# A window-attention and two-expert block on one core: 64x64 products, gates spread by DMA, GpSimd sharing the gate products, and a new order of every engine

## The chip, the cores and the metric

The kernel runs on one core of a Trainium2 chip. The time is the device time of one execution in microseconds (us); lower is better. TensorE (PE), VectorE (DVE), ScalarE (ACT), GpSimd (POOL) and SyncE (SP, which here issues every DMA) each take their own list of instructions in order, and wait for each other through semaphores.

## The reference

The input x is 4 images of 64 channels, 128 by 128, float32. Two layers follow each other, both with a residual.

```
x = x + conv(ln_c(x))            # attention in windows of 8x8 tokens, 4 heads of 16 channels
    qkv  = ln_c(x)^T @ w_qkv.T
    attn = softmax(q k^T / 4 + bias[head])        # 64x64 for each window and head
    out  = (attn v) @ w_proj.T + b_proj
t = t + ffn(ln_t(t))             # t: x by tokens
    p = softmax(ln_t(t) @ router_w + router_b); the two largest, scaled to sum to one
    out = sum over the two of p_k * (ln_t(t) @ expert_w[e_k] + expert_b[e_k])
```

There are 8 experts of 64 by 64. No token is gathered: all 8 experts are applied to every token, each with the token's gate (zero for six of them).

## The kernel before, in words

A strip is 8 rows of two images: 64 channels of image 0 on partitions 0 to 63, of image 1 on 64 to 127, and 1024 tokens, which are 16 windows of 64 tokens. There are 32 strips. Each has two halves (chunks) of 512 tokens. The kernel is a software pipeline written out by hand: one step works on four strips at once (`pre`, `att`, `old`, `moe` at lines 526, 1004 and their like: normalisation with queries and keys, attention, router, experts), every step has 16 slots, and each engine has its own table of what to do in which slot. `steps` (line 232) writes out the first 7 steps, runs a loop of 6 rounds with 4 steps each, and writes out the last ones.

What one strip takes on each engine:

- **Queries and keys.** `split_product` (462): for each of the two and each half, three products 128x128x512 in fp32r, high and low parts of the input against high and low parts of the weights. ACT makes the high part (633), POOL the low part (774).
- **Scores.** `scores` (374, 378), for each of 8 units of two windows: the bias as one fp32r product of 512 columns, and two fp32 products of 256 columns. The weights on 128 partitions hold queries of both images in a block form (`qbd`), the keys are spread over four masked copies (`kex`, made by DVE at 996). Each unit has a PSUM bank of its own, two in all (banks 0 and 1).
- **Softmax.** DVE takes the row maximum (879) and subtracts (882), 512 columns at a time, ACT takes the exponent (587), PE transposes (388), ACT copies back (595), PE multiplies with the values (404) and with ones (410), ACT turns the sums into inverses (602, 604), DVE normalises (889).
- **Projection** (417), residual on POOL (767), router (436, 439), transposes of the logits (446).
- **Top two.** DVE does both picks in a chain of small instructions (`pick`, 920 to 924, and around it), then POOL splits the gates into bf16 parts (791 to 811), PE transposes them (455), DVE copies them to `gT` (1045).
- **Experts.** For each of 16 items (2 halves, 4 expert pairs, 2 images) PE spreads two rows of gates over 128 partitions with a bf16 product of 512 columns (`gates_wide`, 502), DVE multiplies this PSUM bank with `xd` (899; `xd` is the strip with one image on both halves of the partitions, copied by four DMAs at 319), and PE multiplies with two experts at once (`experts`, 514: 128 rows, 64 columns of the array). The two images sit on the two column halves of the array. The expert bias is two bf16 products (511), `finish` (907) adds the residual, and one DMA stores the strip (325).

Every matrix product of an ordinary fp32 operand shows as two matmul records and two weight loads in the trace, one of fp32r or bf16 as one.

## Time and profile before

| | |
|---|---|
| median of 3 runs | 1445.26 us (1443.87 to 1445.51) |
| span of the profiled execution | 1442.2 us |
| busy: PE, PEld (weight loads) | 1343.6 us (93%), 749.6 us |
| busy: DVE | 1161.9 us (81%) |
| busy: ACT | 862.6 us (60%) |
| busy: POOL | 356.8 us (25%) |
| DMA | 72.89 MB, queue q1 17.6% of 16 engines |

The span is what the profiler saw of one execution, from the first instruction to the last; the run's time is some 3 us longer. Busy times overlap across engines. A group "x1024 | 284.7, 621" says that 1024 instructions kept the engine busy for 284.7 us together while one took 621 ns: matmuls are pipelined, and those on different columns of the array overlap. What a group costs on the path is therefore better read from the chain of waits, in which each piece is given from its start to the start of what came next.

### The profile page before, as it was taken

How to read it: one execution, taken by the hardware profiler on the slowest of the kernel's cores; microseconds unless marked ns; L12 is line 12 of the kernel's file. 1: busy time of each engine (PE TensorE's matmuls, PEld its weight loads, DVE VectorE, ACT ScalarE, POOL GpSimd, SP SyncE). 2: the span in 40 equal slices, each digit the busy share in tenths (PEclk: the TensorE clock that was granted, in tenths of full speed). 3: DMA queues.
4: the chain of work that ended last, by engine and by line, in shares of the span. 5: the costliest groups of instructions: out<-in, count | busy, mean ns of one | idle time of the engine just before them, and what ended most of it. 6: DMA issues, size and time to landing. Idle time of an engine off the chain costs nothing.

```text
span 1442.2 us, 32800 instructions
## 1 busy us (share of the span) xinstructions
PE 1343.6 (93%) x11179; PEld 749.6 (52%) x11332; DVE 1161.9 (81%) x2398; ACT 862.6 (60%) x1729; POOL 356.8 (25%) x488
## 2 busy tenths in 40 slices
PE   5779999999998999989999999989999899999987
PEld 3555555555554555555555555545555555555531
DVE  4468888888887888878888788878888788888774
ACT  2576666566665666656666566656666566666530
POOL 2013222331232232122233132222123223213221
PEclk6899999999999999999999999999999999999998
DMA  4011211212221211221121222121222121221110
GB/s 156 1 45 30 60 40 50 60 31 60 60 60 32 60 45 45 60 61 45 45 60 31 60 60 59 35 57 30 60 60 60 31 60 40 51 60 45 45 44 30
DMA packets 20931, 72.89 MB, mean 51 GB/s; under 512 B 3600, under 2 KB 3856, under 8 KB 20624
## 3 DMA queue, kind: packets, MB, share of 16 engines
q1 hardware_dynamic: 20752, 70.60, 17.6%
q8 instruction: 101, 1.65, 0.5%
q14 instruction: 78, 0.64, 0.1%
HBM read 20.25 MB, written 16.78 MB: 26 GB/s over the span
## 4 chain that ended last, share of the span: by engine, by line
PE 69%; ACT 10%; DVE 10%; issue 9%; POOL 1%; DMA 1%; DVEq 0%; ACTq 0%; SPq 0%; POOLq 0%
PE bank L378 14%; PE bank L514 12%; PE bank L388 7%; PE bank L462 6%; PE bank L502 5%; ACT vbd L680 5%; PE bank L417 4%; PE bank L374 4%; PE bank L404 4%; DVE z L899 3%; PE bank L410 2%; PE bank L491 2%; PE bank L484 2%; PE bank L436 2%; DVE mx L879 2%
## 5 line engine op out<-in xcount | busy, mean ns | idle before, releaser
L899 DVE TENSOR_TENSOR z<-bank,xd 128x512 f32<-128x512 f32 x512 | 329.2, 683 | 15.4 <-PE bank L502 9.3
L514 PE MATMUL bank<-z,wcen 128*64 128x512 f32 x1024 | 284.7, 621 | 4.6 <-issue 0.3
L587 ACT ACTIVATE probs<-shifted 128x512 f32<-128x512 f32 x256 | 161.5, 631 | 208.0 <-DVE shifted L882 205.7
L378 PE MATMUL bank<-kex,qbd 128*128 128x256 f32 x1024 | 269.2, 386 | 0.0
L879 DVE TENSOR_REDUCE mx<-bank 128x8 f32<-128x512 f32 x256 | 176.1, 688 | 108.9 <-PE bank L378 107.4
L378 PEld LDWEIGHTS bank<-kex,qbd 128*128 128x128 f32 x1024 | 198.8, 194 | 25.6
L767 POOL TENSOR_TENSOR tt<-prj,xs 128x512 f32<-128x512 f32 x64 | 81.2, 1268 | 457.6 <-DVE z L899 287.9
L882 DVE TENSOR_TENSOR shifted<-bank,mx 128x512 f32<-128x512 f32 x256 | 177.1, 692 | 9.8
L388 PE MATMUL bank<-cst,probs 128*128 128x128 f32 x1024 | 157.7, 277 | 24.9 <-issue 16.8
L595 ACT ACTIVATE pt<-bank 128x512 f32<-128x512 f32 x256 | 150.7, 589 | 46.0 <-PE bank L388 43.0
L388 PEld LDWEIGHTS bank<-cst,probs 128*128 128x128 f32 x1024 | 124.5, 142 | 77.2 <-issue 38.9
L404 PEld LDWEIGHTS bank<-pt,vbd 128*32 128x32 f32 x4096 | 72.4, 109 | 153.8 <-issue 143.5
L502 PE MATMUL bank<-gT,select 128*128 128x512 bf16 x359 | 139.9, 393 | 11.0 <-DVE z L899 6.0
L774 POOL TENSOR_TENSOR xr_low<-xr,xr_high 128x512 fp32r<-128x512 f32 x64 | 81.6, 1274 | 224.9 <-ACT xr_high L633 224.9
L996 DVE TENSOR_SCALAR kex<-kr,cst 128x512 f32<-128x512 f32 x256 | 123.8, 546 | 8.1 <-ACT kr L669 7.1
L502 PEld LDWEIGHTS bank<-gT,select 128*128 128x128 bf16 x512 | 49.4, 98 | 150.7 <-issue 102.9
L374 PE MATMUL bank<-bias_hl,tile_id 128*128 128x512 f32 x256 | 124.2, 485 | 0.7 <-DVE bias_hl L872 0.7
L680 ACT ACTIVATE vbd<-bank 64x256 f32<-64x256 f32 x256 | 96.7, 378 | 32.9 <-PE bank L491 27.3
L404 PE MATMUL bank<-pt,vbd 128*32 128x64 f32 x4096 | 109.6, 225 | 1.0 <-DVE onrm L889 0.8
L791 POOL TENSOR_TENSOR ga<-oh,g 128x128 f32<-128x128 f32 x32 | 13.0, 406 | 367.9 <-DVE g L964 367.9
L514 PEld LDWEIGHTS bank<-z,wcen 128*64 128x64 f32 x1024 | 53.2, 135 | 88.8 <-DVE z L899 43.4
L640 ACT ACTIVATE qbd<-bank 64x512 f32<-64x512 f32 x128 | 75.2, 587 | 16.0 <-PE bank L462 14.4
(116 smaller groups left out, 1998.2 us busy)
## 6 DMA issues: line engine op xcount, KB each, us to landing
xd<-tt SPq DMA_DIRECT2D x128, 256.0 KB, 4.0
xs<-in_x SPq DMA_DIRECT2D x32, 512.0 KB, 4.8
out<-ob SPq DMA_DIRECT2D x32, 512.0 KB, 3.1
kex<-in_rel SPq DMA_DIRECT2D x1, 2048.0 KB, 9.4
tt<-in_select SPq DMA_DIRECT2D x1, 512.0 KB, 8.9
cst<-in_consts SPq DMA_DIRECT2D x1, 359.0 KB, 2.8
tt<-in_weights SPq DMA_DIRECT2D x1, 336.0 KB, 3.1
wproj<-in_proj SPq DMA_DIRECT2D x1, 64.0 KB, 8.2
```

Of the source, the lines that this page charges most:

```text
L374: mm(b, tile_id[:, :], dup(bias_hl[:, :, :].rearrange("p h k -> p (h k)")), start=True, stop=False, skip_group_check=True)
L378: last = mm(b[:, 256 * j:256 * j + 256], qbd[s.buf(2)][:, w, :, :].rearrange("p a q -> p (a q)"), kex[s.buf(2)][:, w, :, :].rearrange("p h ...
L388: last = nc.tensor.transpose(bank[:, PT_BANK, 128 * j:128 * j + 128], probs[u % 2][:, j // 2, 128 * (j % 2):128 * (j % 2) + 128], cv("ident"))
L404: last = mm(bank[q:q + 32, OD_BANK, N * w4:N * w4 + N], vbd[s.buf(2)][:, 2 * u + wl, q:q + 32], pt[g % 2][:, w4, j, a, :], start=True, sto ...
L502: mm(bank[:, G_BANK[n % 2], :], select[:, 4 * a + j, :], gT[s.buf(2)][:, c * CH:(c + 1) * CH], start=True, stop=True).then_inc(g_full, 1)
L514: mm(bank[64 * a:64 * a + 64, Y_BANK, :], wcen[:, WE + C * j:WE + C * j + C], z[n % 4][:, :], start=False, stop=(j == 3), skip_group_check ...
L587: af(probs[u % 2][:, :, :].rearrange("p w k -> p (w k)"), shifted[u % 2][:, :, :].rearrange("p g k -> p (g k)"), ACT.Exp).then_inc(exp_don ...
L595: af(pt[g % 2][:, 2 * (u % 2):2 * (u % 2) + 2, :, :, :].rearrange("p w j a q -> p (w j a q)"), bank[:, PT_BANK, :], ACT.Copy).then_inc(pt_ ...
L680: af(dst[:, :, :, h, :], src[:, :, :, h, :], ACT.Copy).then_inc(v_ready, 1)
L879: red(mx[u % 2][:, :], b, axis=AX_X, op=ALU.max).then_inc(max_done, 1)
L882: tt_(shifted[u % 2][:, :, :], b, mx[u % 2][:, :].unsqueeze(2).broadcast_to([P, 8, N]), op=ALU.subtract).then_inc(shift_done, 1)
L899: tt_(z[n % 4][:, :], bank[:, G_BANK[n % 2], :], xd[s.buf(2)][:, a, c * CH:(c + 1) * CH], op=ALU.mult).then_inc(z_ready, 1)
```

## The change

Almost every instruction is rewritten. What it does:

- **64x64 products.** `wcen`, `wproj` and the new `wex` are used in 64x64 blocks. `swapped` (queries and keys), `project` and `experts` each issue four products of 64 rows, 64 columns and 512 columns of data, one for each quarter of the array, with the two row halves writing different banks. Queries and keys are plain fp32: the split into high and low parts is gone, and with it the instructions on ACT and POOL.
- **Scores.** `kex` and `qbd` go. The queries come out with the windows' halves on the partitions; products of 32 rows and 64 columns, 128 columns of data, go to two banks (the "two score banks" are now one pair, filled by a left half, `scores_left`, and after it a right half, `scores_right`, which uses the other row groups). ACT writes the keys in two masked copies (`move_k`) where DVE wrote four.
- **Softmax** works on four groups of 1024 columns in place of eight units of 512. It is done in place in `probs`.
- **Gates by DMA.** Three transposes of 128 columns replace eight. ACT copies them to `gsb`, a DMA writes them to a DRAM buffer `gates_dram`, and for each expert two DMAs read one row into 64 partitions of `gz`. `gates_wide` is gone. Six small DMAs bring rows for the expert bias (`grow`).
- **Gate products.** `gz` times the strip, 128x1024 with both inputs in SBUF, eight for each strip: experts 1, 4 and 7 on POOL, the other five on DVE. There is one `gz` buffer for each expert, so an expert's next gates are loaded when its product is done.
- **Order.** Eight pipeline stages in place of four, one written list for each engine and step (39 steps for 32 strips; 11 written out, a loop of 5 rounds with 4 steps, 8 written out).
- **Store.** `ob` now has image-independent halves, stored with four DMAs whose runs are 64 numbers (256 bytes) long; `xd` gives way to `tx`, half as large.

```diff
+            def write_gates(s):
+                sp.wait_ge(gsb_ready, s.count(1, 1))
+                sp.dma_start(gates_dram[s.buf(4)].rearrange("s r (x p) -> (r x) s p", p=P),
+                             gsb[:, :, :]).then_inc(gates_written, 16)
+            def load_gate_rows(s):
+                sp.wait_ge(gates_written, s.count(16, 16))
...
+            def spread_gates(s, e):
+                wait(sp, e_done, s.count(E, e + 1, lag=1))
+                for a in range(2):
+                    sp.dma_start(gz[64 * a:64 * a + 64, e, :],
+                                 gates_dram[s.buf(4), 0, E * a + e, :].partition_broadcast(64)
+                                 ).then_inc(gz_loaded[e], 16)
...
-                for w, v in ((0, 1), (1, 0), (0, 0)):
-                    last = mm(bank[:, PRE, :], wqk_hl[w][:, at:at + P], chunk(xr_hl[v], c), start=(w, v) == (0, 1),
-                              stop=(w, v) == (0, 0), skip_group_check=True)
+                for x in range(2):
+                    for a in range(2):
+                        last = mm(bank[64 * x:64 * x + 64, PRE + a, :], wcen[64 * a:64 * a + 64, at + 64 * a:at + 64 * a + 64],
+                                  xr[s.buf(2)][64 * a:64 * a + 64, x, :, :].rearrange("p w n -> p (w n)"),
+                                  start=True, stop=True)
...
+                        for hp in range(2):
+                            r = 2 * x + hp
+                            last = mm(bank[N * j:N * j + N, S_BANK + hp, 256 * x + 128 * ii:256 * x + 128 * ii + 128],
+                                      qs[32 * r:32 * r + 32, a, w, :],
+                                      km[32 * r:32 * r + 32, CW * a + w, :, :].rearrange("p m k -> p (m k)"),
+                                      start=False, stop=(ii == 1), skip_group_check=True)
...
-                mm(bank[:, G_BANK[n % 2], :], select[:, 4 * a + j, :], gT[s.buf(2)][:, c * CH:(c + 1) * CH],
-                   start=True, stop=True).then_inc(g_full, 1)
...
-                mm(bank[64 * a:64 * a + 64, Y_BANK, :], wcen[:, WE + C * j:WE + C * j + C], z[n % 4][:, :],
-                   start=False, stop=(j == 3), skip_group_check=True).then_inc(e_done, 1)
+                for x in range(2):
+                    for a in range(2):
+                        last = mm(bank[64 * x:64 * x + 64, Y_BANK + a, :], wex[64 * a:64 * a + 64, e, :],
+                                  gz[64 * a:64 * a + 64, e, x * CH:(x + 1) * CH],
+                                  start=False, stop=(e == E - 1), skip_group_check=True)
+                last.then_inc(e_done, 1)
...
+        POOL_Z = [1, 4, 7]
+        DVE_Z = [e for e in range(E) if e not in POOL_Z]
...
+            def gated(s, e):
+                dve.wait_ge(gz_loaded[e], s.count(32, 32))
+                tt_(gz[:, e, :], gz[:, e, :], tt[s.buf(4)][:, :, :].rearrange("p x t -> p (x t)"),
+                    op=ALU.mult).then_inc(z_dve, 1)
```

The order on TensorE, in the middle of a step of the kernel before. L388 are the transposes, L374 and L378 the scores of one unit, L502 a spread of gates, L514 a pair of expert products, L484 a spread of the inverse deviations, L404 and L410 values and denominators:

```order
L388 MATMUL bank<-cst,probs 128x128 x4
L374 MATMUL bank<-bias_hl,tile_id 128x512
L378 MATMUL bank<-kex,qbd 128x256 x2
L502 MATMUL bank<-gT,select 128x512
L514 MATMUL bank<-z,wcen 64x512 x2
L484 MATMUL bank<-var_hl,spread 128x512
L404 MATMUL bank<-pt,vbd 32x64 x8
L410 MATMUL bank<-pt,cst 32x256 x4
L502 MATMUL bank<-gT,select 128x512
```

And with the change, from the expert bias on (L581). L593 are the products of one expert (x4) or three (x12), L437 keys and then queries, L491 and L476 bias and one half of the scores of a group:

```order
L581 MATMUL bank<-grow,eb 128x512 x2
L428 MATMUL bank<-var_hl,spread 128x512 x2
L509 MATMUL bank<-cst,probs 128x128 x4
L476 MATMUL bank<-km,qs 64x128 x8
L593 MATMUL bank<-gz,wex 64x512 x4
L437 MATMUL bank<-xr,wcen 64x512 x4
L593 MATMUL bank<-gz,wex 64x512 x12
L437 MATMUL bank<-xr,wcen 64x512 x4
L526 MATMUL bank<-pt,vbd 32x64 x16
L509 MATMUL bank<-cst,probs 128x128 x4
L533 MATMUL bank<-pt,cst 32x256 x4
```

No spread of gates stands between the experts any more, and experts, keys and queries of the same shape now follow each other.

The end of a step on VectorE with the change. L1000 and L1007 are maximum and subtraction, L1021 a gate product (experts 0 and 2 at the end, of the strip whose gates were made in this step), L1015 the normalisation, and L975 and L980 (the variance) open the next step:

```order
L1021 TENSOR_TENSOR gz<-gz,tt 128x1024
L1015 TENSOR_TENSOR onrm<-bank,rden 128x256
L1021 TENSOR_TENSOR gz<-gz,tt 128x1024
L1000 TENSOR_REDUCE mx<-bank 128x16
L1007 TENSOR_TENSOR probs<-bank,mx 128x1024
L1021 TENSOR_TENSOR gz<-gz,tt 128x1024
L975 TENSOR_TENSOR var<-bank,msq 64x512
L980 TENSOR_SCALAR var<-var 64x512
```

Before, a gate product read a PSUM bank that PE filled; now it reads what a DMA has written, and the maximum of the third score group is queued behind one.

One step on SyncE with the change (before, it issued six DMAs: `xs`, four `xd`, `out`). The write at L304 waits for the gates of this step, the six rows at L312 for that write:

```order
L340 DMA out<-ob 64x8x64 x4
L329 DMA tx<-tt 64x512 x4
L304 DMA gates_dram<-gsb 128x3x128
L312 DMA grow<-gates_dram 8x2x512 x6
L320 DMA gz<-gates_dram 64x1024 x8
L299 DMA xs<-in_x 128x1024
L320 DMA gz<-gates_dram 64x1024 x8
```

The first eight `gz` are experts 0 to 3 of the strip just routed, the last eight (experts 4 to 7 of the same strip) belong to the next step.

## Rows read from the trace of the kernel before

**Rows 1.** The page: span, busy time, slices and TensorE's granted clock.

```profile
span 1442.2 us, 32800 instructions
PE 1343.6 (93%) x11179; PEld 749.6 (52%) x11332; DVE 1161.9 (81%) x2398; ACT 862.6 (60%) x1729; POOL 356.8 (25%) x488
PEclk6899999999999999999999999999999999999998
q1 hardware_dynamic: 20752, 70.60, 17.6%
```

**Rows 2.** Stretches of one step: busy us (instructions) of each engine, clock, DMA.

```profile
666.60:708.20 41.60, 40.54 (x344) 22.86 (x346) 35.79 (x74) 26.86 (x55) 11.24 (x16) 1.00 0.19 52
708.20:749.80 41.60, 40.73 (x345) 22.77 (x347) 35.79 (x74) 27.00 (x56) 11.06 (x16) 1.00 0.19 52
```

**Rows 3.** Chain in order of time: start us, us until the next, what.

```profile
722.22 0.21 PE bank L502
722.44 1.01 PE bank L514 x4
...
723.88 0.36 PE bank L404 x16
724.24 0.43 PE bank L410 x8
724.67 0.55 PE bank L484
725.22 0.44 PE bank L388 x4
725.66 0.23 PE bank L374
725.89 0.86 PE bank L378 x4
...
731.79 0.59 PE bank L511 x2
732.38 1.01 PE bank L514 x4
733.39 0.89 PE bank L462 x3
```

**Rows 4.** The same chain before and at a return of the loop.

```profile
445.68 0.90 PE bank L491 x8
...
448.87 3.48 issue
452.35 0.67 PE bank L388 x4
453.03 0.43 PE bank L374
453.45 1.71 PE bank L378 x4
```

**Rows 5.** Groups of instructions by line and shape: DVE and ACT, and POOL's.

```profile
L899 DVE TENSOR_TENSOR z<-bank,xd 128x512 f32<-128x512 f32 x512 | 329.2, 683 | 15.4 <-PE bank L502 9.3 <-remote 2.9 <-DVE oh L924 1.1
L889 DVE TENSOR_TENSOR onrm<-bank,rden 128x256 f32<-128x256 f32 x128 | 53.1, 414 | 5.4 <-ACT rden L604 5.3
L921 DVE TENSOR_TENSOR eq<-L,m 128x128 f32<-128x128 f32 x64 | 18.7, 292 | 3.0 <-DVE m L920 1.0
L604 ACT ACTIVATE rden<-rden 128x256 f32<-128x256 f32 x128 | 53.4, 417 | 4.1
L587 ACT ACTIVATE probs<-shifted 128x512 f32<-128x512 f32 x256 | 161.5, 631 | 208.0 <-DVE shifted L882 205.7
L767 POOL TENSOR_TENSOR tt<-prj,xs 128x512 f32<-128x512 f32 x64 | 81.2, 1268 | 457.6 <-DVE z L899 287.9 <-ACT prj L690 169.7
L791 POOL TENSOR_TENSOR ga<-oh,g 128x128 f32<-128x128 f32 x32 | 13.0, 406 | 367.9 <-DVE g L964 367.9
L795 POOL TENSOR_TENSOR gp<-ga,gb 128x128 bf16<-128x128 f32 x32 | 21.6, 674 | 0.0
```

**Rows 6.** Timeline of SP's own queue: start us, us for the issues.

```profile
0.75 0.40 SPq L286 DMA_DIRECT2D cst<-in_consts  x1
...
5.24 0.64 SPq L306 DMA_DIRECT2D tt<-in_select  x1
```

**Rows 7.** DMA groups: KB each, median us from issue to landing.

```profile
xd<-tt SPq DMA_DIRECT2D x128, 256.0 KB, 4.0
cst<-in_consts SPq DMA_DIRECT2D x1, 359.0 KB, 2.8
```

**Rows 8.** Timeline: start us, us, engine; DVE and POOL side by side.

```profile
702.11 2.23 DVE L996 TENSOR_SCALAR kex<-kr,cst 128x512 f32<-128x512 f32 x4
719.21 1.67 DVE L996 TENSOR_SCALAR kex<-kr,cst 128x512 f32<-128x512 f32 x4
...
702.20 0.71 POOL L795 TENSOR_TENSOR gp<-ga,gb 128x128 bf16<-128x128 f32 x1
1411.16 0.45 POOL L795 TENSOR_TENSOR gp<-ga,gb 128x128 bf16<-128x128 f32 x1
```

**Rows 9.** Timeline of the setup, DVE and PE: one-hot tables, bias products, bias.

```profile
12.52 4.62 DVE L844 TENSOR_SCALAR xd<-kex,cst 128x4096 bf16<-128x4096 int32 x2 [2.48 <-DMA kex<-in_rel]
17.19 1.03 PE L347 MATMUL bank<-tb,xd 128*64 128x12 bf16 x32 [7.25 <-DVE xd L844]
35.74 0.28 DVE L867 COPY probs<-bank 128x128 f32<-128x128 f32 x1
37.99 0.42 DVE L872 TENSOR_TENSOR bias_hl<-probs,bias_hl 64x256 fp32r<-64x256 f32 x1
```

More of the change, by code:

```diff
@@ L224, in __init__, with strips @@
                 self.c, self.n, self.inner = c, n, inner
-            def strip(self, off):
-                return Strip(self.c + off, self.n, self.inner)
+            def strips(self):
+                return [Strip(self.c - k, self.n, self.inner) for k in range(LAST_STAGE + 1)]
         class Strip:
@@ L255, in steps @@
         def steps(run):
-            first, last = -1, STRIPS + 1
-            lo = 6
-            n = (STRIPS - 1 - lo) // U
-            for i in range(first, lo):
+            last = STRIPS - 1 + LAST_STAGE
+            lo = LAST_STAGE + 4
+            n = (STRIPS - lo) // U
+            for i in range(lo):
                 run(Step(i, 0, False))
@@ L314, in _ @@
[L314 to L325 removed]
+                s = st.strips()
@@ new lines, in score_tiles @@
+            def score_tiles(s, g, x):
+                a = g // 2
+                for ii in range(2):
+                    for j in range(2):
+                        w = 4 * (g % 2) + 2 * ii + j
+                        for hp in range(2):
[4 more added lines that the diff above has]
+                                      start=False, stop=(ii == 1), skip_group_check=True)
+                return last
@@ new lines, in _ @@
+                s = st.strips()
+                if s[7].on:
+                    experts(s[7], 7)
+                if s[4].on:
+                    values(s[4], 1)
+                if s[5].on:
+                    router(st, s[5])
+                if s[4].on:
+                    denominators(s[4], 0)
+                    transposes(s[4], 2)
+                if s[5].on:
+                    transpose_logits(st, s[5])
+                if s[4].on:
+                    scores_left(s[4], 3)
+                if s[6].on:
+                    expert_bias_rows(s[6])
@@ new lines, in _ @@
+                if s[3].on:
+                    spread_std(st, s[3])
+                if s[4].on:
+                    transposes(s[4], 3)
+                    scores_right(s[4], 3)
+                if s[6].on:
+                    experts(s[6], 0)
+                if s[3].on:
+                    keys(st, s[3])
+                if s[6].on:
+                    experts(s[6], 1)
+                    experts(s[6], 2)
+                    experts(s[6], 3)
+                if s[3].on:
+                    queries(st, s[3])
@@ new lines, in _ @@
+                if s[6].on:
+                    experts(s[6], 4)
+                if s[4].on:
+                    project(st, s[4])
+                if s[3].on:
+                    scores_right(s[3], 2)
+                    transposes(s[3], 1)
+                    values(s[3], 0)
+                if s[2].on:
+                    channel_sums(st, s[2])
+                if s[6].on:
+                    experts(s[6], 5)
+                    experts(s[6], 6)
+                if st.c == 0:
+                    bias_rows()
```

1131 lines of the change are left out of this document (570 added, 561 removed).

## The prediction

> **What bounds the kernel now.** I read the page first: PE is busy 93% of the span, DVE 81%, and TensorE's granted clock is at 0.9 or more of its full 2.4 GHz in all but the first slices [rows 1]. Then the stretches of single steps: a step is 41.6 us, of which PE is busy 40.5 to 40.7, DVE 35.8, ACT 26.9, POOL 11.1 [rows 2]. Then the chain in order of time, in which piece follows piece on PE with no wait between [rows 3]. The kernel is bound by PE's own work. As a check, all the work of one strip, priced from the chain. Scores are 8 x (0.23 + 0.86) = 8.7, transposes 8 x 0.44 = 3.5, values and denominators 8 x 0.36 + 4 x 0.43 = 4.6, queries and keys 4 x 0.89 = 3.6, expert pairs 8 x 1.01 = 8.1, 16 spreads of gates at 0.21 (0.27 with changes of shape) = 4.3, two bias pairs 1.2; I add 7.7 for the rest (values' input 2 x 0.90 [rows 4] = 1.8, projection 2.0, deviations 1.0, router 1.0, sums 0.9, transposes of logits and gates 1.0). Together 41.7, against 41.6 measured. So the pieces of the chain are prices that add up to the step.
>
> At a return of the loop there are 3.48 us without an issue, and the scores behind it take 1.71 in place of 0.86, half the clock [rows 4]. Such a return costs some 4.9 us more than another step.
>
> **PE after the change.** I take the price of a piece of 512 fp32 columns from the pair L514, two products on different columns of the array: 1.01 us for both [rows 3]. L378, which has as many columns of data in a row (two products of 256), takes 0.86, so 0.15 of the 1.01 is the change of shape. The decisive unknown is what four products on the quarters cost. No product before uses fewer than 128 rows, so this trace does not show row halves side by side. Bounds: as the column halves do (0.86 for four), or one row half after the other (1.72 for four). I take the first, because the nearest row is a pair of column parts that run fully beside each other, and the two row halves here write different banks; the second is a rival below.
>
> - Eight experts, keys, queries and projection: 11 fours. In the new order experts 0 to 3 stand around keys and queries, 4 beside projection, 5 to 7 together, so three of them pay 1.01 and eight 0.86: 9.9 us.
> - Scores: four groups of two bias products (0.46) and two halves. A half is eight products of 128 columns on four parts of the array, two after each other, as many columns as L410 (0.43), plus 0.15 for the shape: 1.16. Together 6.5.
> - Unchanged: transposes 3.5, values and denominators 4.6, router 1.0, sums 0.9, logits' transposes 0.4, and 2.0 for the values' input (now 32 small products). 12.4.
> - Deviations 0.7, three gate transposes 0.35, expert bias as fp32r 0.6: 1.6. The spreads of gates are gone.
>
> The sum is 30.4 us for a strip.
>
> **DVE, ACT, POOL after the change.** From 256 to 512 columns a DVE instruction grows from 414 to 683 ns [rows 5], 1.05 ns a column, so 1024 columns are 1.22 us. DVE has 15 of these (5 gate products, 4 maxima, 4 subtractions, scaling, finish) = 18.3, four normalisations 1.7, variance 1.8, and the chain of some 22 small instructions at 0.17 to 0.29 with the waits between them, 6.5: 28.3 us. ACT grows by 0.84 ns a column (417 to 631), 1.06 for 1024: 12 of them 12.5, eight copies of 512 4.7, the rest 7.5: 24.7. POOL: (1268 - 406)/384 = 2.24 ns a column, so a gate product is 2.4 us; three, two residuals and seven-tenths of the old gate work (3.1) are 12.8. None of these sums exceeds PE's, but DVE is close behind.
>
> **DMA.** Before, 70.6 MB took 17.6% of 1442 us [rows 1], 3.6 us for a MB. Per strip there will be 16 x 0.262 (gates) + 3 x 0.52 (load, `tx`, store) + 0.3 = 6.1 MB: 22 us, no bound. The price lies in the latency. SP issues 32 DMAs in a step, and each keeps its queue for 0.40 to 0.64 [rows 6]; I take 0.45. The new stores have runs of 256 bytes, which no row shows; nothing waits for a store but `ob` two steps later, so they cost nothing on the path, and 2 us of DMA time even at half the rate.
>
> **The new path.** DVE's list is a ring: from the top of a step through the top-two picks and the gates, then out through POOL, PE, ACT and DMA, and back into DVE at the gate product of expert 0, behind which stands the third group's softmax and expert 2. Its length:
>
> 1. DVE from the variance to the gates, all that is queued there: 14.8 of work (five 1.22, variance 1.8, normalisation 0.4, the small chain 6.5) and 1.2 of waits for ACT and PE: 16.
> 2. POOL places the gates 3.1, three transposes with their latency 0.55, ACT's copy 0.55: 4.2.
> 3. The write to DRAM until it has landed, by the nearest small load [rows 7]: 2.8.
> 4. Six row loads and two spreads issued, 8 x 0.45 = 3.6, and landing. `xd`, of the same size, has 4.0 from issue; the bound below is 2.8 [rows 7]. I take 3.0 behind the last issue: 6.6.
> 5. Gate product, maximum, subtraction, gate product: 4.9.
>
> That is 34.5 us, longer than PE's 30.4. One more thing is added. DVE's new gate products have two inputs in SBUF, as has POOL's. In the trace DVE's four L996, SBUF to SBUF, took 2.23 us while POOL worked and 1.67 when it did not, and POOL's L795 0.71 against 0.45 [rows 8]: the two hold each other up. POOL will be busy 12.8 of some 35 us. Bounds: nothing, or that each DVE instruction of this kind waits for half of a 2.4 us product in a third of the cases, 0.4 each, some 2.5 us on the ring. I take 0.5, since only part of the ring meets POOL at work. A step is then **35.0 us**.
>
> On the same point the Trainium skill, SBUF — State Buffer, section "SBUF: two separate sides", says that the shared pair of ports is an exclusive lock, held for a whole instruction, between GpSimd and a DVE instruction with two SBUF inputs. By that rule the ring would be some 37 to 38 us in place of 35.
>
> **The sum.** Setup until the bias tables are there: 31 us. Before, the one-hot tables were ready at 17.1, the 256 small products took 1.03 for 32, and the bias 2.6 after the last [rows 9]; now the tables come some 2 us later, behind four more loads, and all of it stands before the first strip: 19.1 + 8.2 + 2.6 = 30, and one for the hand-overs. Steps 3 to 6 fill the pipeline: 25, 27, 30, 34 = 116. Steps 7 to 34, 28 of them, at 35.0: 980. The last four: 26 (attention's end and the gates), 27 (the ring without attention), 10 (seven experts) and 7 (the last expert, finish, a store of 3 to 4) = 70. Four returns of the loop at 4.9: 20. Together a span of 1217 us, against 1442.2; with the 3.1 between span and median before, **1220 us**, 15.6% less. The setup, filling and emptying are my estimates from the order of the work and the same rows, good to 20 us.
>
> **Rivals.**
>
> *PE stays the bound.* The latency of step 3 and 4 of the ring is shorter, or hidden, and PE's 30.4 with a few waits gives 31 to 33.5: 1217 - 28 x 1.5 to 4.0 = 1105 to 1175, centre 1145. For it: the pieces of the chain added up to the step before. Against: everything between gates and expert 0 is new and serial.
>
> *DVE and POOL block each other.* At the top of a step POOL takes two gate products in a row (expert 1, then expert 4), while DVE has the guard of the variance, expert 3 and the small chain. If a DVE instruction must wait for the end of a 2.4 us product, the variance chain comes 2.3 us late, the scaled input with it, and the keys. Expert 5 behind expert 7 costs more. With 36.5 to 40 a step: 1262 to 1360, centre 1300. For it: both engines lost time beside each other [rows 8]. Against: in these rows DVE lost 0.14 us for each instruction, not a whole one of POOL's.
>
> *Slower: row halves do not run side by side.* Each of the 11 fours costs 0.86 more, each of 8 score halves 0.43 more: 9.5 + 3.4 = 12.9, so PE needs 43.3 a step, above the ring. 31 + 116 + 25 + 28 x 43.3 + 80 + 20 = 1484: 1487 us, 3% slower. It turns slower than before once a step exceeds 43 us, that is when hardly anything of the row halves overlaps. For it: no row shows it. Against: column parts do overlap, down to quarters (L404, 16 records in 0.36).
>
> **How the numbers follow.** The forecast (33.5 to 36.5 a step) has 0.44, PE as the bound 0.24, blocking 0.23, the slow row halves 0.08, and 0.01 for no change. So faster by over 0.2% (about what a measurement can tell from no change) 0.91, within 0.2% 0.01, slower 0.08. The range takes in the forecast's 1175 to 1262, nearly all of the first rival and the larger part of the second: 1110 to 1330.
>
> **What would show it.** A step of 35 us; PE busy some 88%, DVE 85%; four products L593 in 0.86 to 1.01, records 5 to 10 ns apart (1.7 and more: the slower rival). DVE's wait before L1021 ended by the DMA into `gz`, some 2 to 3 us in a step: right; no such wait: the first rival. L1021 on DVE well over 1.22 us, or DVE's small instructions stretched while POOL runs: the second. I am wrong if the waits of a step end on something I gave no price, such as ACT's place in the order.

## The result, and the profile after it

| | before | after |
|---|---|---|
| median of the runs | 1444.6 us (1442.8 to 1445.5) | 1325.8 us (1318.8 to 1332.2) |
| span of the profiled execution | 1442.2 us | 1316.9 us |
| mean granted clock | 0.98 | 0.93 |

The ratio is 0.918, with an interval from 0.914 to 0.921: 8.2% less time, where 15.6% was forecast. The direction held, the size was off by 106 us. The time lies inside the range (1110 to 1330) by only 4 us, and far outside what the forecast's own steps allowed (1175 to 1262): it is inside because the range was drawn wide enough for the rivals.

The page of the kernel after, for [rows 1] and the groups of [rows 5]. First the busy time of each engine with its share of the span, then TensorE's clock in 40 slices, the DMA queue (packets, MB, share of 16 engines), then groups of instructions (busy us, mean ns | idle before them and what ended it):

```profile
span 1316.9 us, 40785 instructions
PE 1124.7 (85%) x16486; PEld 600.8 (46%) x16486; DVE 938.3 (71%) x1431; ACT 753.4 (57%) x1185; POOL 417.4 (32%) x359
PEclk9988889898998988999899989998888899998877
q1 hardware_dynamic: 143040, 200.28, 64.0%
L1021 DVE TENSOR_TENSOR gz<-gz,tt 128x1024 f32<-128x1024 f32 x160 | 242.2, 1515 | 156.7 <-DMA gz<-gates_dram 156.7
L903 POOL TENSOR_TENSOR gz<-gz,tt 128x1024 f32<-128x1024 f32 x96 | 229.5, 2391 | 224.4 <-DMA gz<-gates_dram 224.4
L1000 DVE TENSOR_REDUCE mx<-bank 128x16 f32<-128x1024 f32 x128 | 156.5, 1223 | 71.9 <-PE bank L476 69.1
L740 ACT ACTIVATE probs<-probs 128x1024 f32<-128x1024 f32 x128 | 134.9, 1054 | 17.8 <-DVE probs L1007 17.5
```

No engine is busy all the time now. TensorE went from 93% to 85%, DVE from 81% to 71%. Both engines that multiply gates wait for the transfers into `gz`: 157 us on DVE, 224 us on GpSimd. The prices of the 1024-column instructions came out as estimated (1.22 and 1.05). But a gate product on DVE took 1515 ns on average, not 1220, and TensorE's clock, at 0.9 or more in nearly all slices before, is lower in many slices.

I measure a step from one variance (L975) to the next. The 27 steps from 170.3 to 1192.1 us last 37.8 each: the four with a return of the loop 40.6, the 23 others 37.4. One of these others is 37.06 long (703.38 to 740.44). Here is DVE's timeline of it (start, duration, instruction, [idle before it and what ended that]):

```profile
703.38 0.69 DVE L975 TENSOR_TENSOR var<-bank,msq 64x512 f32<-64x512 f32 x1
704.11 0.42 DVE L980 TENSOR_SCALAR var<-var 64x512 f32<-64x512 f32 x1
...
707.25 0.69 DVE L985 TENSOR_TENSOR var_hl<-var,var_hl 64x512 fp32r<-64x512 f32 x1
707.97 2.25 DVE L1062 TENSOR_TENSOR mq<-st_ 128x16 f32<-128x16 f32 x1
710.26 0.18 DVE L1063 TENSOR_TENSOR vr<-st_,mq 128x16 f32<-128x16 f32 x1
...
719.75 0.17 DVE L1101 TENSOR_TENSOR g<-ed,g 128x16 f32<-128x16 f32 x1
...
733.38 1.23 DVE L1021 TENSOR_TENSOR gz<-gz,tt 128x1024 f32<-128x1024 f32 x1 [2.95 <-DMA gz<-gates_dram]
734.52 1.22 DVE L1000 TENSOR_REDUCE mx<-bank 128x16 f32<-128x1024 f32 x1
735.87 1.22 DVE L1007 TENSOR_TENSOR probs<-bank,mx 128x1024 f32<-128x1024 f32 x1
739.18 1.23 DVE L1021 TENSOR_TENSOR gz<-gz,tt 128x1024 f32<-128x1024 f32 x1 [2.09 <-DMA gz<-gates_dram]
740.44 0.69 DVE L975 TENSOR_TENSOR var<-bank,msq 64x512 f32<-64x512 f32 x1
```

GpSimd's and SP's timelines of the same step, and the landing times of the DMAs (KB, median us from issue to landing):

```profile
707.82 2.38 POOL L903 TENSOR_TENSOR gz<-gz,tt 128x1024 f32<-128x1024 f32 x1 [5.55 <-DMA gz<-gates_dram]
...
722.18 0.53 POOL L897 TENSOR_TENSOR gp_hl<-gsum,gp_hl 128x128 fp32r<-128x128 f32 x1
724.17 0.40 SPq L304 DMA_DIRECT2D gates_dram<-gsb  x1
726.25 1.99 SPq L312 DMA_DIRECT2D grow<-gates_dram  x6
728.36 4.95 SPq L320 DMA_DIRECT2D gz<-gates_dram  x8
gz<-gates_dram SPq DMA_DIRECT2D x512, 256.0 KB, 6.8
gates_dram<-gsb SPq DMA_DIRECT2D x32, 192.0 KB, 2.1
```

These rows give the five terms of the ring one by one. The last column cuts all 23 steps without a return at the same instructions and gives the means:

| term | forecast | this step | 23 steps |
|---|---|---|---|
| (1) DVE, variance to gates | 16 (+0.5 for blocking) | 703.38 to 719.92: 16.5, blocking included | 16.7, of it blocking 1.0 |
| (2) placing, transposes, copy | 4.2 | to 724.17: 4.2 | 4.4 |
| (3) write until landed | 2.8 | to 726.25: 2.1 | 2.1 |
| (4) rows, first pair, landing | 6.6 | to 733.38: 7.1 | 7.3 |
| (5) product, softmax, product | 4.9 | to 740.44: 7.1 | 6.9, of it blocking 1.0, wait 0.9 |

Four of five are within 0.7. Term (5) missed by 2.2 in this step, nearly all of it the wait of 2.09 us for expert 2's gates. This step is not typical in that: over the 23 steps the wait is 0.9 us, and 1.0 us more of term (5) is DVE's products running beside GpSimd's (1515 ns on average where 1220 was expected). "Blocking" is here, and in all that follows, the time by which DVE's instructions are longer than the same ones in a kernel whose GpSimd has no products.

Expert 2's gates are the third pair of transfers in SP's order, and the pairs arrive one after the other. How fast, the stretches around another step's end show (us, PE, PEld, DVE, ACT, POOL busy, granted clock, DMA share, GB/s):

```profile
575.00:588.50 13.50, 10.43 (x139) 4.15 (x137) 8.52 (x10) 7.43 (x11) 5.84 (x3) 1.00 0.91 224
588.50:595.30 6.80, 6.80 (x48) 4.67 (x48) 4.80 (x10) 3.85 (x8) 2.27 (x1) 0.50 1.04 226
```

While the spreads run, the DMA engines are full at some 225 GB/s, so a pair of transfers of 256 KB takes 0.524 MB / 225 = 2.3 us. My 22 us a strip (before: 3.6 us for a MB) was called "no bound", since it fits into a step. But once the gates are placed, SP issues four pairs in one burst (728.36 to 733.31, x8), and the first three are in the ring.

The first row of DVE's L1062 shows the other loss: 0.18 us of work on 16 columns took 2.25 us, from 707.97 to 710.22, while GpSimd's product ran from 707.82 to 710.20. DVE's instruction ended when GpSimd's did. This is the rule that the Trainium skill gives in SBUF — State Buffer, section "SBUF: two separate sides", an exclusive lock for a whole instruction; here the trace agrees. The step of 37.8 us lies in what I had estimated by that rule (37 to 38), but in part by luck: without the returns it is 37.4, and blocking puts 2.0 us a step on the ring (1.0 in term 1, 1.0 in term 5), which alone makes 34.5 + 2.0 = 36.5.

The second stretch above has the clock at 0.50, that is 1.2 GHz. TensorE's timeline around it:

```profile
585.14 0.66 PE L509 MATMUL bank<-cst,probs 128*128 128x128 f32 x4
588.45 1.07 PE L563 MATMUL bank<-cst,lg 128*128 128x128 f32 x4 [2.65 <-ACT lg L775]
589.18 1.20 PE L491 MATMUL bank<-bias_hl,tile_id 128*128 128x512 f32 x2
590.31 1.13 PE L476 MATMUL bank<-km,qs 32*64 32x128 f32 x16
...
595.29 1.10 PE L593 MATMUL bank<-gz,wex 64*64 64x512 f32 x8
596.22 1.03 PE L437 MATMUL bank<-xr,wcen 64*64 64x512 f32 x8
597.08 2.75 PE L593 MATMUL bank<-gz,wex 64*64 64x512 f32 x24
599.67 1.09 PE L437 MATMUL bank<-xr,wcen 64*64 64x512 f32 x8
600.69 0.65 PE L526 MATMUL bank<-pt,vbd 128*32 128x64 f32 x32
```

Two things are read here. TensorE had waited 2.65 us for ACT's copy of the logits; then 6.8 us went at half clock (one half of the scores, L476, 1.13 in place of 0.67). There are 29 such stretches, 188 us together; before, 9 with 36 us over the same part of the span (from 56 us on). And a "four" of 64x64 products (x8 records) costs 0.86 within a row of three experts (2.59 from 597.08 to 599.67) and up to 1.02 ahead of another shape (599.67 to 600.69): the row halves do run side by side, as forecast.

### The profile page after: what moved, and what is told of

It is laid out like the page before. It is cut to its first block, busy times and chain, and to the rows that moved or that the text cites. A ratio compares the mean times of both kernels' runs of the same rounds, so it can differ in the third digit from the quotient of the medians.

```text
span 1316.9 us, 40785 instructions
## 1 busy us (share of the span) xinstructions
PE 1124.7 (85%) x16486; PEld 600.8 (46%) x16486; DVE 938.3 (71%) x1431; ACT 753.4 (57%) x1185; POOL 417.4 (32%) x359
## 4 chain that ended last, share of the span: by engine, by line
PE 37%; issue 23%; DMA 13%; POOL 10%; SPq 6%; DVE 5%; ACT 4%; POOLq 0%; ACTq 0%; DVEq 0%
DMA gz<-gates_dram 11%; PE bank L593 8%; POOL gz L903 6%; PE bank L476 6%; PE bank L509 5%; SPq L320 4%; PE bank L437 3%; PE bank L491 3%; PE bank L526 3%; POOL tt L877 2%; PE bank L533 2%; DMA gates_dram<-gsb 2%; SPq L312 2%; PE bank L464 2%; PE bank L428 1%
## 5 line engine op out<-in xcount | busy, mean ns | idle before, releaser
L1021 DVE TENSOR_TENSOR gz<-gz,tt 128x1024 f32<-128x1024 f32 x160 | 242.2, 1515 | 156.7 <-DMA gz<-gates_dram 156.7
L903 POOL TENSOR_TENSOR gz<-gz,tt 128x1024 f32<-128x1024 f32 x96 | 229.5, 2391 | 224.4 <-DMA gz<-gates_dram 224.4
L593 PE MATMUL bank<-gz,wex 64*64 64x512 f32 x2048 | 259.6, 623 | 26.4 <-issue 24.2
L1000 DVE TENSOR_REDUCE mx<-bank 128x16 f32<-128x1024 f32 x128 | 156.5, 1223 | 71.9 <-PE bank L476 69.1
L476 PE MATMUL bank<-km,qs 32*64 32x128 f32 x4096 | 183.7, 297 | 0.3
L1007 DVE TENSOR_TENSOR probs<-bank,mx 128x1024 f32<-128x1024 f32 x128 | 156.8, 1225 | 11.5
L476 PEld LDWEIGHTS bank<-km,qs 32*64 32x64 f32 x4096 | 117.7, 140 | 92.9 <-issue 88.8
L740 ACT ACTIVATE probs<-probs 128x1024 f32<-128x1024 f32 x128 | 134.9, 1054 | 17.8 <-DVE probs L1007 17.5
L593 PEld LDWEIGHTS bank<-gz,wex 64*64 64x64 f32 x2048 | 71.3, 138 | 160.5 <-issue 160.4
L725 ACT ACTIVATE km<-bank,hmask 128x1024 f32<-128x1024 f32 x64 | 67.8, 1110 | 93.8 <-PE bank L437 93.8
L491 PE MATMUL bank<-bias_hl,tile_id 128*128 128x512 f32 x256 | 98.5, 468 | 10.2 <-ACT qs L718 6.8
L533 PE MATMUL bank<-pt,cst 128*32 128x256 f32 x1024 | 84.9, 397 | 3.1 <-issue 3.1
L437 PE MATMUL bank<-xr,wcen 64*64 64x512 f32 x512 | 73.1, 639 | 11.2 <-ACT km L725 7.3
```

The costliest lines, as they stand in the source:

```text
L476: last = mm(bank[N * j:N * j + N, S_BANK + hp, 256 * x + 128 * ii:256 * x + 128 * ii + 128], qs[32 * r:32 * r + 32, a, w, :], km[32 * r:32 ...
L491: mm(bank[:, S_BANK + hp, :], tile_id[:, :], bias_hl[:, 2 * hp:2 * hp + 2, :].rearrange("p h k -> p (h k)").unsqueeze(1).broadcast_to([P, ...
L593: last = mm(bank[64 * x:64 * x + 64, Y_BANK + a, :], wex[64 * a:64 * a + 64, e, :], gz[64 * a:64 * a + 64, e, x * CH:(x + 1) * CH], start= ...
L740: af(v, v, ACT.Exp).then_inc(exp_done, 1)
L903: tt_(gz[:, e, :], gz[:, e, :], tt[s.buf(4)][:, :, :].rearrange("p x t -> p (x t)"), op=ALU.mult).then_inc(z_pool, 1)
L1000: red(mx[g % 2][:, :], two_banks(S_BANK).rearrange("p (c k) -> p c k", k=N), axis=AX_X, op=ALU.max).then_inc(max_done, 1)
```

## The experiments

The theories: **the ring** (the step is the length of the path through DVE, GpSimd, TensorE, ACT and DMA), **the rate** of the transfers within it, **the blocking** of DVE and GpSimd, and **TensorE's stalls** with their lost clock. For each kernel I give the median of its runs, and from its profiled execution the time, the mean of 27 steps like those above, DVE's wait for `gz`, and the blocking on DVE: the time of its instructions beyond what the same ones take on the median in the kernel "e6" below (the gate product: 1215 ns).

| kernel | median us | profiled | step | DVE waits for `gz` | blocking on DVE |
|---|---|---|---|---|---|
| the change | 1325.8 | 1318.8 | 37.8 | 157 | 80 |
| e1: order 0, 2, 1, 3 | 1315.4 | 1311.6 | 37.5 | 130 | 100 |
| e2: and five rows late | 1264.4 | 1259.5 | 35.9 | 88 | 122 |
| e4: gates from a fixed block | 1281.0 | 1300.0 | 37.9 | 7 | 135 |
| e5: all products on DVE | 1269.8 | 1280.0 | 36.6 | 98 | 9 |
| e6: e5 and five rows late | 1220.5 | 1217.7 | 34.6 | 45 | 15 |
| e8: e4, all products on DVE | 1237.7 | 1236.0 | 35.7 | 3 | 18 |
| e9: half of each spread | 1293.2 | 1300.4 | 37.6 | 88 | 125 |
| e12: e5, half of each spread | 1197.6 | 1197.9 | 33.9 | 47 | 13 |

The profiled execution of the change lasted 7 us less than its median, those of e5, e9 and e4 10, 7 and 19 us more, so the steps of these three are somewhat too long beside that of the change. Without the profiled execution, e4's median is 1279.2.

### The order of the transfers (e1, e2)

e1 puts expert 2's spread ahead of expert 1's:

```diff
                     spread_gates(s[5], 0)
-                    spread_gates(s[5], 1)
                     spread_gates(s[5], 2)
+                    spread_gates(s[5], 1)
                     spread_gates(s[5], 3)
```

> Only the order of issue on SP changes: experts 0, 2, 1, 3 in place of 0, 1, 2, 3. Ring theory (the step is the length of the ring from the gates through DRAM and the DMA back into VectorE, whose last wait is for expert 2): expert 2 lands 2.2 us earlier, VectorE's 2.1 us wait before its last gate product goes, and a step falls by up to 2.1 us: some 1265 to 1290 us. Rival, the rate of the DMA as such (all 16 gate loads of a step are needed, whichever comes first): no change, 1325 within 8 us.

Measured: 1315.4 us, ratio to before 0.913 [0.910, 0.916], only 10 us less than the change, far from the ring's range and next to the rival's. But the range was worked out from the one step above, with its wait of 2.1 us. In the 23 steps the wait for expert 2 was 0.9 on average. It is gone in e1: DVE's wait for `gz` fell by 27 us, and term (5) from 6.9 to 5.2. Most of this was paid back in blocking: term (1) grew from 16.7 to 18.0. With expert 1's gates later, GpSimd multiplies at the top of the step, and two DVE groups stretch:

```profile
L980 DVE TENSOR_SCALAR var<-var 64x512 f32<-64x512 f32 x32 | 44.1, 1378 | 1.1
L1070 DVE TENSOR_TENSOR Ls<-Lr,rs 128x128 f32<-128x128 f32 x32 | 29.2, 914 | 0.7 <-ACT rs L786 0.7
L1021 DVE TENSOR_TENSOR gz<-gz,tt 128x1024 f32<-128x1024 f32 x160 | 223.0, 1395 | 130.4 <-DMA gz<-gates_dram 130.2
```

The guard of the variance takes 0.42 us alone and 1.38 here. It stands at the head of the ring.

e2 adds to that order: one of the six row loads keeps its place, the other five go behind the third pair.

```diff
                     write_gates(s[5])
-                    load_gate_rows(s[5])
+                    load_gate_rows(s[5], False)
                     spread_gates(s[5], 0)
...
+                    load_gate_rows(s[5], True)
                     spread_gates(s[5], 3)
```

> As e1_order02, and five of the six small row loads for the expert bias are issued behind expert 1, before expert 3. Ring theory: expert 0 is issued 1.6 us earlier as well, so a further 1.6 us of a step or less, until another wait ends last: 1225 to 1260 us. DMA-rate rival: as before, since the loads are the same.

Measured: 1264.4 us, 0.877 [0.873, 0.882], 61 us less than the change and 51 less than e1, 4 us above the ring's range. L312 took 1.99 us for six rows, so five are 1.66 us that leave the ring in each of 32 steps: 53 us. Time inside the ring does count. The blocking (122 us) grew once more, most of all on the guard of the variance:

```profile
L984 DVE TENSOR_SCALAR var<-var 64x512 f32<-64x512 f32 x32 | 54.5, 1704 | 1.1
```

### The ring cut (e4)

The spreads and rows read a fifth block of `gates_dram`, which the setup writes once; they wait for no gates of the step. The write of the gates moves behind the spreads. The kernel leaves out that the experts use this token's gates.

```diff
-                                 gates_dram[s.buf(4), 0, E * a + e, :].partition_broadcast(64)
+                                 gates_dram[4, 0, E * a + e, :].partition_broadcast(64)
```

> The spreads and the rows read a fifth DRAM slot that is written once at the start, so the kernel leaves out that the experts use this token's gates; the gates are still made and written, but nothing waits for them. All instructions and all bytes stay. Ring theory: the ring is cut, and a step falls to what TensorE or VectorE need, 31 to 34 us: 1130 to 1200 us. DMA-rate rival: the loads still take 25 us of a step with their queue full, the step stays near 37: 1290 us or more. Lock rival (VectorE and GpSimd hold each other up): the step keeps some 4 us of such waits and comes out near 35 to 36: 1230 to 1270 us.

Measured: 1281.0 us, 0.885 [0.879, 0.890], in none of the three ranges. The ring alone, as I had it, was refuted as the whole account: DVE's wait for gates is gone (7 us), and the time fell by only 45 us. What grew is the blocking (135 us) and DVE's wait for scores:

```profile
L1006 DVE TENSOR_REDUCE mx<-bank 128x16 f32<-128x1024 f32 x128 | 156.8, 1225 | 177.2 <-PE bank L482 174.4
L1068 DVE TENSOR_TENSOR mq<-st_ 128x16 f32<-128x16 f32 x32 | 37.2, 1164 | 1.0
L986 DVE TENSOR_SCALAR var<-var 64x512 f32<-64x512 f32 x32 | 52.2, 1630 | 1.1
```

### Blocking (e5, e6, e8)

e5 takes the three products from GpSimd and puts them into DVE's list, each next to its neighbours (the rest of the edit moves the calls):

```diff
-        POOL_Z = [1, 4, 7]
+        POOL_Z = []
```

> All eight gate products on VectorE (expert 1 between 0 and 2, 4 before 5, 7 behind 6); GpSimd has only gates and residuals. Lock theory: the three products cost VectorE 3.7 us and give back some 4 us (gate products at 1.22 in place of 1.52 us, and the small instructions that stood 2 us behind a GpSimd product): 1310 to 1335 us, and VectorE's gate products at 1.22 to 1.3 us. If the lock costs little, 2 to 3.7 us a step are added: 1390 to 1440 us.

Measured: 1269.8 us, 0.879 [0.875, 0.883], 56 us less than the change, though DVE got 96 x 1.22 = 117 us of work more. The loss by blocking is larger than I had put on record for it: 1269.8 is 40 us below that range. The rows for those above:

```profile
L1015 DVE TENSOR_TENSOR gz<-gz,tt 128x1024 f32<-128x1024 f32 x256 | 312.7, 1250 | 98.3 <-DMA gz<-gates_dram 98.1
L974 DVE TENSOR_SCALAR var<-var 64x512 f32<-64x512 f32 x32 | 13.6, 424 | 1.1
L1056 DVE TENSOR_TENSOR mq<-st_ 128x16 f32<-128x16 f32 x32 | 5.6, 176 | 1.0
```

e6 is e5 with the five row loads behind expert 2's spread (SP's order 0, 1, 2, rows, 3).

> The two edits that brought 61 us and 56 us, made together: five of the six row loads stand behind expert 2's spread, and all eight gate products are on DVE. If they attack different losses (the one the place of the transfers in the ring, the other the mutual blocking of DVE and GpSimd), the gains add up: 1326 - 61 - 56 = 1209, so 1200 to 1225. If both only shorten the same wait (DVE for the gate of expert 2 in the ring), the second gain is mostly in the first: 1245 to 1262. DVE then has some 29.7 us of work a strip, which at 33 steps, with fill and emptying, allows no less than about 1160.

Measured: 1220.5 us, 0.847 [0.844, 0.851]. 105 us less than the change, against 61 + 56 = 117: the two edits attack nearly separate losses. It computes what the reference asks and is the fastest such kernel of this study, 8% faster than the change.

e8 is e4 with all products on DVE.

> As the kernel whose spreads read a block of DRAM that is written once in the setup (1281 us; its outputs do not use the gates), but with all eight products on DVE. So neither the ring nor GpSimd's products are there. If what was left in that kernel was DVE and GpSimd blocking each other, this one gives 1170 to 1210. If it was the DMA traffic (200 MB, and stalls in the supply of TensorE's instructions), it stays at 1250 to 1290.

Measured: 1237.7 us, 0.858 [0.854, 0.861], between the two ranges: 43 us less than e4, so blocking was the larger part of what e4 had left, but slower than e6 by 17 us, although nothing waits for gates. DVE waits 131 us for scores. TensorE has ten gaps of 1.7 to 4.5 us before it issues, two in each pass of the loop, 28 us in all; e6 has four of 2.9 to 5.1, 15 us, at the loop's returns. But e8's 27 steps are 31 us longer than e6's (35.7 against 34.6 each), so these 13 us are not all of it. What the rest is, and why the second gap arises, was not tried.

### The rate (e9, e12)

Each spread moves only 512 of its 1024 tokens, with the same number of transfers and waits. The products work on old data in their second half, so the experts' part of every second chunk is left out:

```diff
-                    sp.dma_start(gz[64 * a:64 * a + 64, e, :],
-                                 gates_dram[s.buf(4), 0, E * a + e, :].partition_broadcast(64)
+                    sp.dma_start(gz[64 * a:64 * a + 64, e, 0:512],
+                                 gates_dram[s.buf(4), 0, E * a + e, 0:512].partition_broadcast(64)
```

> The changed kernel, but each spread of a gate moves only the first 512 of its 1024 tokens (128 KB in place of 256 KB; the second half of the gate products works on old data, so the experts' part of every second chunk is not computed). Number of transfers, waits and order are as they were. If the rate of the transfers prices step (5) of the ring (2.2 us for a pair of transfers), the wait of DVE for experts 0 and 2 shrinks by some 3 us a step: 1225 to 1250. If the latency of issue and landing prices it, or the blocking of DVE and GpSimd, it stays at 1290 to 1320.

Measured: 1293.2 us, 0.893 [0.887, 0.898]. 33 us less, in the range of the rival and not in that of the rate. The waits tell more. DVE's wait for `gz` fell by 69 us, and the blocking rose by 45:

```profile
L1021 DVE TENSOR_TENSOR gz<-gz,tt 128x1024 f32<-128x1024 f32 x160 | 257.9, 1614 | 87.6 <-DMA gz<-gates_dram 87.5
L980 DVE TENSOR_SCALAR var<-var 64x512 f32<-64x512 f32 x32 | 40.2, 1255 | 1.1
```

So the same edit without GpSimd's products, e12:

> The kernel with all eight products on DVE (1270 us), with the half-size spreads (128 KB in place of 256 KB; the second half of the products works on old data, so the experts' part of every second chunk is not computed). GpSimd's products, which took back the gain of the half-size spreads in the changed kernel (blocking 80 to 125 us on DVE), are not there. If the rate of the transfers is in the ring, DVE's wait for them (98 us) falls to 30 to 45 and the time to 1215 to 1230, as with the late row loads. If issue and landing are what is waited for, the time stays at 1255 to 1270.

Measured: 1197.6 us, 0.829 [0.828, 0.830], 72 us less than e5, more than the rate's range. With both causes varied, the four kernels are:

| | whole spreads | half spreads |
|---|---|---|
| three products on GpSimd | 1325.8 | 1293.2 |
| all on DVE | 1269.8 | 1197.6 |

Alone, the edits bring 33 and 56 us, together 128. While GpSimd multiplies, data that come sooner let its products meet other DVE instructions, and half of the gain goes back.

Not all of the 72 us is the time until a spread has landed. At the four returns of the loop e5 has long waits for nothing that the profile shows ("issue"), on TensorE and on DVE (us in all, times, longest), and e12 has none over 0.6 us. The first two rows are e5's, the last is e12's:

```profile
L593 PE MATMUL bank<-gz,wex 64*64 64x512 f32 x2048 | 259.1, 623 | 20.5 <-issue 18.9
DVE var L969 <- issue: 14.4, 4, 4.3
L593 PE MATMUL bank<-gz,wex 64*64 64x512 f32 x2048 | 250.6, 606 | 8.7 <-DVE gz L1015 8.7
```

The same shows in e6. Its 23 steps without such a wait last 33.6 to 35.1 us, all 27 of e12 33.6 to 35.2; the other four last 38.3 to 38.6. Whether the fuller DMA engines cause the longer returns, no run separates.

TensorE is now the bound. The steady stretches of the change, and of e12 (same columns as above), 27 steps each:

```profile
170.00:1192.00 1022.00, 920.93 (x13690) 493.07 (x13689) 783.96 (x1189) 633.59 (x999) 349.19 (x297) 0.94 0.70 164
```

```profile
170.00:1086.00 916.00, 875.68 (x13693) 464.09 (x13689) 811.50 (x1270) 634.17 (x999) 137.47 (x216) 1.00 0.43 122
```

TensorE is busy 96% of e12's steady part, at full clock: 875.7 / 27 = 32.4 us a strip. In the change the same instructions took 920.9, 45 us more. Its half-clock stretches hold 101 us of busy TensorE in this window; at full clock that work would take some 50 us less, so the half clock accounts for the difference.

### TensorE's stall and the place of DVE's products (e10, e11, e3, e7)

In the change TensorE waits 62 us for ACT's copy of the logits, because ACT first waits for DVE's variance. e10 swaps the two on ACT, e11 does the same to e6:

```diff
+                if s[5].on:
+                    move_logits(s[5])
                 if s[3].on:
                     log_var(s[3])
-                if s[5].on:
-                    move_logits(s[5])
```

> The changed kernel, but ACT copies the router's logits before it takes the logarithm of the variance, for which it waits for DVE. TensorE's wait for that copy (62 us in all) goes, and with it many of the stretches at half clock that follow an idle TensorE (188 us in all). If the step is set by the ring through DVE and the transfers, TensorE's stalls only fill slack: 1310 to 1326, no gain beyond 1%. If lost clock is a cost of its own, 1270 to 1300.

Measured: 1313.2 us, 0.911 [0.908, 0.915], 0.95% less than the change. The waits for the copy are gone. In their place stand waits for DVE, 25 us for its variance, and those for the low part of the variance grew from 11 to 49:

```profile
PE bank L563 <- DVE var L974: 25.1, 23, 1.5
PE bank L428 <- DVE var_hl L984: 48.8, 31, 4.9
```

Half-clock stretches fell from 188 to 134 us (from 58 us on), and TensorE's busy time in the whole from 1124.7 to 1105.3. So 19 us of TensorE's time came back, and the run gained 12.6, near the lower end of what the ring allowed (1310); it stayed 13 us above the range of the rival, lost clock as a cost of its own. DVE's wait for `gz` stayed (153 us). The blocking on DVE rose from 80 to 100 us meanwhile, so the clock's own cost is not told by this run either.

> The same edit of ACT's order on the fastest kernel so far (five row loads late, all eight products on DVE, 1220 us), in which TensorE is busy 89% and waits 33 us for that copy. Here TensorE is near its limit, so its stalls should count whichever theory holds: 33 us of waits and part of the 72 us at half clock go, 1185 to 1205. No change (1215 to 1222) would mean that DVE sets the step there too.

Measured: 1229.0 us, 0.850 [0.847, 0.853]: 9 us slower than e6, or the same within the spread of both (1218 to 1230 and 1224 to 1241). A miss. The wait went to the next late thing: `PE bank L432 <- DVE var_hl` has 45.8 us, where e6 had 33 for the logits and 9 for that. TensorE got past the logits sooner and then waited for DVE's part of the same variance.

e3 (on e2) and e7 (on e6) take products from the end of the ring into the next step. The edit of e3 on DVE (e7 moves expert 2 alone, and expert 0 behind the third softmax of the same step):

```diff
                 if s[6].on:
-                    gated(s[6], 3)
+                    gated(s[6], 0)
                 if s[5].on:
                     move_logits(s[5])
                 if s[3].on:
                     low_part(s[3])
+                if s[6].on:
+                    gated(s[6], 2)
+                    gated(s[6], 3)
...
-                if s[5].on:
-                    gated(s[5], 0)
...
-                if s[5].on:
-                    gated(s[5], 2)
```

> As the kernel with five late row loads (1264 us), but DVE's own products 0 and 2 are moved out of the end of the ring to the head of the next step, behind finish and the low part of the variance. The wait of DVE for a gate transfer in the ring (88 us in all there) goes. Ring theory: the step is then set by DVE's work and its blocking, some 31 to 33 us: 1190 to 1225. Rival: DVE's products at the head of a step stand in front of the router's chain and meet GpSimd's products, and TensorE's experts come later in the step: 1250 to 1290.

> The 1220 us kernel with DVE's product for expert 0 behind the third group's softmax instead of ahead of it, and the one for expert 2 in the head of the next step. The wait of DVE for a transfer in the ring (45 us there) goes. If that wait still sets the step: 1185 to 1205. If TensorE then gets expert 2 late, or the softmax chain was the longer one: 1220 to 1250, as the step's head on DVE grows by 1.2 us.

Measured (e3's profiled execution lasted 1% longer than its median): e3 1318.1 us, 0.911 [0.908, 0.913], 54 us slower than e2 and worse than its rival's range. e7 1242.5 us, 0.860 [0.859, 0.862], 22 slower than e6, as its rival said. In both DVE's wait for `gz` fell (88 to 16, 45 to 27), and other waits took more: in e3

```profile
DVE mx L1004 <- PE bank L480: 162.4, 93, 11.4
DVE ob L1033 <- PE bank L597: 54.6, 23, 8.1
DVE es L1102 <- ACT ed L795: 34.6, 32, 3.0
```

(waits: us in all, times, longest). The products now stand in front of the small chain that makes the next gates and of the scaled input for the keys, and TensorE waited 73 us for the latter. The head of the ring cannot hide them; they had only changed their place in it.

## Why the prediction was right in direction and off in size

The mechanism was right: the 64x64 products bring TensorE's work below the ring, and the ring sets the step. Its length was forecast too short, 35.0 us where the 23 steps without a return have 37.4. Of these 2.4 us, 1.5 are blocking and 0.9 is a wait that had no price.

- **Blocking is the largest term that failed.** It was priced at 0.5 us a step on the ring and took 2.0 (1.0 in term 1, 1.0 in term 5); over all of DVE it was 80 / 32 = 2.5. I averaged over DVE's instructions in [rows 8], where GpSimd's instructions were short. With 2.4 us products, one small DVE instruction with two inputs in SBUF that begins during one waits for its end. Giving the three products to GpSimd cost more than it brought (e5). The result lies in the range of that rival (1262 to 1360), to which I gave 0.23; its mechanism is about half of the miss (56 us of 106, by e5).
- **Term (5)**: 4.9 forecast, 6.9 measured. Half of the difference is the blocking above. The other half is the wait for expert 2's gates, 0.9 us, which I took as there when DVE came to it. They are the third pair of a burst in which the engines are full, at 2.3 us a pair. The total of 22 us a strip was the wrong test; the test was what of the burst lies ahead of the one waited for. e2 shows what row loads ahead of the pairs cost, 51 us beyond e1; e12 shows the rate's weight without blocking, at most 72 us, the shorter returns in it.
- **Ring, terms (1) to (4).** Term (3), the write, was 0.7 shorter than forecast and term (4) 0.7 longer. Term (1) without blocking was 15.7 where 16 was forecast, (2) 4.4 for 4.2. Right.
- **PE's pieces.** A four at 0.86 to 1.02 (forecast 0.86 and 1.01), a score half at 0.60 (0.58): right, and the slower rival fell. The sum was too low: 32.4 us a strip in e12, not 30.4. From start to start in e12, the transposes took 4.5 us a strip (3.5 in the sum), bias and scores 7.4 (6.5), the eleven fours 10.4 (9.9); the rest came out as summed.
- **The sum.** The span came out at 1316.9 instead of 1217: the 27 steady steps took 1021.8 in place of 27 x 35 + 20 = 965 (+57), though a return cost 3.2 us more than another step and not 4.9; filling (steps 3 to 6) 140.7 in place of 116 (+25); one step and the last four 124.8 in place of 105 (+20); the setup 29.6 in place of 31. Filling and emptying were priced at full clock. In the first step of filling the keys (L437) took 1.99 us where they take 1.09 later, and the last 27 us had a granted clock of 0.72.
- **PE stays the bound** came true only where both causes were out: in e12, and in e6 between the returns, both with steps of some 33.8 us, above what that rival had (31 to 33.5).
- **What the profile was to show.** The wait before L1021 by the DMA was there: ahead of expert 0 it was 2.95 in the step shown and 3.2 on average, ahead of expert 2 it was 0.9 more. PE busy 88% and DVE 85% were too high (85% and 71%).

Half clock had no price in the sum. It is a consequence here: TensorE's steady work was 45 us longer than in e12, but as the ring set the step, part of this may have fallen into slack. How much, no run separates: e10 gave TensorE 19 us back and gained 12.6, with 20 us more of blocking.

## What to carry to other kernels

When a value goes through DRAM to come back broadcast, count the bytes and the issues that stand ahead of the first and the last transfer that the ring waits for, not the total of a step; then put everything else (here five row loads of 32 KB) behind them. Before giving elementwise work to GpSimd, look at what DVE runs meanwhile: a long GpSimd product costs a DVE instruction with two inputs in SBUF that meets it up to its own whole length (one that reads PSUM lost nothing here), so that moving 117 us of work back to DVE made this kernel 56 us faster. Read a term of a ring from many steps: the one step shown here had a wait of 2.1 us where the mean was 0.9, and e1's range was off by that. And when an edit removes a wait and brings little, compare the mean durations of the groups, not only the waits: in e1 and e9 the gain had gone into longer instructions.

## What the runs showed of the hardware that I had not expected

- A DVE instruction of 16 columns (0.18 us) takes 2.25 us if it starts 0.15 us after a GpSimd product of 2.38 us, and ends with it. The guard of the variance (L980, L984 in e2; a TENSOR_SCALAR with one SBUF input, 64x512) is held up too: 424 ns alone, 1704 on average in e2. DVE's instructions that read PSUM are not: the maximum and the subtraction stay at 1.22 us in every kernel shown here, and in e2 the variance itself began during a GpSimd product 24 times and lost nothing.
- Four fp32 products on the quarters of the array, two row halves by two column halves, run side by side: 0.86 us from start to start for 512 columns each in a row, up to 1.02 ahead of another shape. Before, two products on column halves took 1.01 ([rows 3]).
- Spreads with 4096-byte packets fill the 16 DMA engines at 225 GB/s. Half the bytes of each spread in as many packets brought the queue's share from 64% to 39% of a shorter span (q1, e12).
- Longer stalls of TensorE at the loop's returns: 4.8 to 7.5 us ahead of L593 at four returns of the change, 24.2 in all, where [rows 4] had 3.48 at one; 8.6 in all in e9 and none over 0.6 in e12, with half of each spread. The cause stays open.
